# The sum that ends softplus: from VectorE to an accumulating DMA on GpSimd's queue

## What is computed

```
dt = softplus(dt @ W_dt.T + b_dt)             # 512 channels, 512 tokens
A  = -exp(A_log)                              # 512 channels, 16 states
for every token t:                            # for each channel, state n
    h[n] = exp(dt[t] * A[n]) * h[n] + dt[t] * B[t][n] * x[t]
    y[t] = sum over n of h[n] * C[t][n]
out = (y + x * D) * silu(res) @ W_out.T
```

## Time and profile before

| | us |
|---|---|
| median of 3 runs | 2991.44 |
| lowest and highest | 2991.06, 2993.72 |
| the profiled execution | 3002.96 |
| its span, first to last instruction | 3001.2 |

### The profile page before, as it was taken

How to read it: one execution, slowest core, us unless ns; L and a number is a source line. 1 busy time by engine, 2 the same in 40 slices (tenths; PEclk the granted TensorE clock), 3 DMA queues, 4 the chain that set the end, 5 groups by cost and what they waited for, 6 DMA issues and landing times.

```text
span 3001.2 us, 37634 instructions
## 1 busy us (share of the span) xinstructions
PE 2462.4 (82%) x12744; PEld 1387.2 (46%) x12744; DVE 1979.7 (66%) x2957; ACT 1852.0 (62%) x3346; POOL 1731.5 (58%) x1416
## 2 busy tenths in 40 slices
PE   5777679998689998998989898988898879866772
PEld 3444457764444454445444544454444544442331
DVE  4778744543366766776767677766767676778887
ACT  3456723346477785766667667775677667755752
POOL 1000054417657786777688759775876686544555
PEclk9888879999899999998989899999999989988896
DMA  4000158854545565545554455446544653366666
GB/s 142 22 18 5 49 167 236 242 174 69 94 116 108 109 142 130 113 99 111 135 113 100 108 129 110 85 95 141 114 86 94 133 110 81 85 134 138 158 158 144
DMA packets 281152, 344.83 MB, mean 115 GB/s; under 512 B 81600, under 2 KB 210510, under 8 KB 280960
## 3 DMA queue, kind: packets, MB, share of 16 engines
q0 software_dynamic: 84224, 176.19, 32.1%
q1 hardware_dynamic: 174224, 144.67, 16.6%
q10 hardware_dynamic: 22512, 21.57, 2.1%
HBM read 198.10 MB, written 26.80 MB: 75 GB/s over the span
## 4 chain that ended last, share of the span: by engine, by line
PE 44%; ACT 17%; issue 13%; DVE 13%; POOL 7%; DMA 4%; SPq 2%; another core or an unknown queue 0%; DVEq 0%; POOLq 0%; ACTq 0%
PE bank L1763 7%; PE bank L1752 6%; PE bank L1714 5%; PE bank L1899 4%; PE bank L1873 3%; PE bank L1928 3%; PE bank L1821 3%; DVE bank L1532 3%; ACT PT L1018 3%; POOL arena L1643 3%; PE bank L1775 3%; ACT Pr L998 2%; POOL acc_sb L1621 2%; DMA arena<-bc_dram 2%; PE bank L1998 2%
## 5 line engine op out<-in xcount | busy, mean ns | idle before, releaser
L1643 POOL TENSOR_TENSOR arena<-arena 128x512 f32<-128x512 f32 x512 | 859.8, 1738 | 169.7 <-DMA arena<-bc_dram 153.5
L1227 DVE TENSOR_REDUCE negmax<-bank 128x1 f32<-128x512 f32 x512 | 341.2, 681 | 258.7 <-PE bank L1752 257.8
L1621 POOL DMA_INDIRECT acc_sb<-ybuf,slot_idx x256 | 422.1, 1649 | 141.5 <-DMA ybuf<-arena 63.4
L1135 ACT ACTIVATE bank<-arena,A_sb 128x512 f32<-128x512 f32 x512 | 356.6, 699 | 223.5 <-DVE arena L1537 187.8
L1649 POOL TENSOR_TENSOR arena<-arena 128x512 f32<-128x512 f32 x192 | 279.0, 1453 | 323.5 <-DVE arena L1532 290.6
L1752 PE MATMUL bank<-Kp,Qp 64*128 64x512 f32 x1024 | 405.6, 683 | 70.5 <-ACT Pr L998 65.6
L1763 PE MATMUL bank<-ident,Pr 128*128 128x128 f32 x2048 | 353.4, 298 | 127.0 <-ACT PT L1018 63.8
L1532 DVE TENSOR_TENSOR_SCAN bank<-bank,arena 128x512 f32<-128x512 f32 x320 | 390.8, 1221 | 90.2 <-ACT bank L1135 53.3
L998 ACT ACTIVATE Pr<-bank,negmax 128x512 f32<-128x512 f32 x512 | 354.4, 692 | 154.8 <-DVE negmax L1227 138.4
L1018 ACT COPY PT<-bank 128x512 f32<-128x512 f32 x512 | 301.3, 588 | 204.9 <-PE bank L1763 189.9
L1763 PEld LDWEIGHTS bank<-ident,Pr 128*128 128x128 f32 x2048 | 228.9, 147 | 306.5 <-issue 106.3
(11 more groups left out here) (213 smaller groups left out, 3883.2 us busy)
## 6 DMA issues: line engine op xcount, KB each, us to landing
arena<-arena POOLq DMA_DIRECT2D x256, 512.0 KB, 5.4
arena<-bc_dram SPq DMA_DIRECT2D x256, 256.0 KB, 4.2
ybuf<-arena ACTq DMA_DIRECT2D x64, 256.0 KB
arena<-in_w_gate SPq DMA_DIRECT2D x64, 128.0 KB
arena<-in_w_up SPq DMA_DIRECT2D x64, 128.0 KB
arena<-in_w_down SPq DMA_DIRECT2D x64, 128.0 KB
arena<-in_X SPq DMA_DIRECT2D x8, 512.0 KB, 7.1
s_sb<-in_X SPq DMA_DIRECT2D x8, 512.0 KB, 9.1
```

The lines of the kernel that those rows point to most:

```text
L1135: act.activation(bank[DECAY[g % 2]][:, :], dt_sb[:, size_slot(b, cb), :], ACT.Exp, scale=A_sb[:, cb, n:n + 1]).then_inc(ssm_decay, 1)
L1227: dve.tensor_reduce(negmax[:, m % RING_STAT:m % RING_STAT + 1], bank[m % RING_S_ATT][:, :], AX.X, ALU.max, negate=True).then_inc(att_max, 1)
L1621: pool.indirect_dma_start(acc_sb[:, i, :], None, ybuf, bass.IndirectOffsetOnAxis(ap=slot_idx[:, b * TILES + i, k:k + 1], axis=0), bounds_c ...
L1643: pool.tensor_tensor(st_sb[:, g % RING_S, :], u_sb[:, size_slot(b, cb), :], B_sb[:, load % RING_BC, :], ALU.mult).then_inc(ssm_input, 1)
```

## The change

ACT now clips at zero when it writes `dt_sb` (Relu in place of Identity). DVE's L1517 is gone. In its place POOL waits for ACT's logarithm and issues, for each block, one DMA that adds 128x512 of `u_sb` onto `dt_sb` (256 KB; two for a part, 32 in all). The decays and DVE's product L1523 wait for these DMAs to land. `state_inputs` has a piece more: the sum stands beside the step that L1517 stood beside, and the product and `ssm_d` stand one step later than they did.

```diff
--- before.py
+++ after.py
@@ state_inputs
                 E.ssm_soft(b, part)
                 yield True
+                E.ssm_add(b, part)
+                yield True
                 E.ssm_u(b, part)
                 yield True
@@
+    def sized(b, part):
+
+        return 16 * (CB * b + sum(SIZE_PARTS[part]))
@@ ACT, ssm_abs
-                act.activation(dt_sb[:, size_slot(b, cb), :], bank[SIDE][:, :], ACT.Identity, bias=chan_sb[:, cb, DCONV + 1:DCONV + 2]).then_inc(ssm_raw, 1)
+                act.activation(dt_sb[:, size_slot(b, cb), :], bank[SIDE][:, :], ACT.Relu, bias=chan_sb[:, cb, DCONV + 1:DCONV + 2]).then_inc(ssm_raw, 1)
@@ ACT, decay
-                    w.wait_ge(ssm_dt, len(SIZE_PARTS) * b + PART_OF[cb] + 1)
+                    w.wait_ge(ssm_dt, sized(b, PART_OF[cb]))
@@ DVE
             def ssm_u(self, b, part):
-                runs, use = size_runs(b, part), len(SIZE_PARTS) * b + part
-                w.wait_ge(ssm_raw, CB * b + sum(SIZE_PARTS[part]))
-                w.wait_ge(ssm_soft, 2 * use + 2)
-                for own, _ in runs:
-                    dt, u = whole(dt_sb[:, own, :]), whole(u_sb[:, own, :])
-                    ins = dve.scalar_tensor_tensor(dt, dt, 0.0, u, ALU.max, ALU.add)
-                ins.then_inc(ssm_dt, 1)
-                w.wait_ge(ssm_dt, use + 1)
+                runs = size_runs(b, part)
+                w.wait_ge(ssm_dt, sized(b, part))
                 w.wait_ge(ssm_xs, CB * (b + 1))
@@ POOL
+            def ssm_add(self, b, part):
+
+                first, count = SIZE_PARTS[part]
+                w.wait_ge(ssm_raw, CB * b + first + count)
+                w.wait_ge(ssm_soft, 2 * (len(SIZE_PARTS) * b + part) + 2)
+                for cb in range(first, first + count):
+                    slot = size_slot(b, cb)
+                    pool.dma_start(dt_sb[:, slot, :], u_sb[:, slot, :], accum_op=ALU.add).then_inc(ssm_dt, 16)
```

More of the change, by code:

```diff
@@ L123, in ssm_soft, with ssm_add @@
     def ssm_soft(self, b, part): pass
+    def ssm_add(self, b, part): pass
     def ssm_u(self, b, part): pass
```

## The result

The changed kernel takes 3024.40 us in the median of 5 runs (3015.32 to 3034.63), beside 2991.44 us (2987.89 to 2997.20, 5 runs) for the kernel before on the same chip. The ratio is 1.0105, 95% interval 1.0076 to 1.0134. The forecast was 2996 us with a range up to 3007 us. The loss has the sign of the rival "POOL held", and it is some seven times the forecast loss of 4.6 us.

A forecast was written before the change was run, and what follows sets the result against it. No one engine was taken to bound it; the chain ran 44% over PE, 17% ACT, 13% DVE. Start +3.3, batch 1 +0.5, batches 2 to 6 -0.5, batch 7 +1.3: +4.6 us on 2991.4, 2996 us; range up to 3007 us.

The forecast's parts named there:

- POOL held: Rival, slower: POOL waits for the logarithm with gather, inputs and products queued behind; 3004 us; chance 0.35, shared with a start above 6 us.
- Batches 3 to 6 read alike: Middle batches: batch 2, part 0 was worked out and taken to stand for the rest; batches 2 to 6 together -0.5 us.
- the ten free parts: Batches 2 to 6, two parts each: L1517 off the chain, dt landed 2.6 us before the product; -0.5 us, between -4 and +2.
- The stretching that I had counted as gone with L1517: DVE: L1517 takes 1.2 us alone, 2.22 or 2.34 us beside POOL's inputs; the excess was to go with it.
- Batch 1, +0.5 us: Batch 1, chain on POOL: POOL's lateness just fits its margin, DVE gains L1517's 2.34 us; +0.5 us, between -3 and +4.
- 6.8 us of margin: Batch 1: step 64's input ended at 1098.8, its scan began at 1105.55; POOL, about 6 us late, was to fit.
- The start, +3.3 us: Batch 0, nothing covers: L1143 2.85 us late by the landing, plus 0.4 us for part 1; bounds +1.5 and +5.
- The landing, 5.4 us: Every part: from the logarithm's end to dt landed, after two DMA issues; 5.4 us, low end 3.9, high end 6.3.
- the 9.6 us of the longest L1659: Longest landing of a 512 KB add in the trace; landings near it would reach DVE at batches 2 to 6 too.
- Batch 7, +1.3 us: Batch 7, DVE on the chain: product waits for landing, then takes 1.22 us, delaying scan 444 and mask; bounds 0 and +2.9.
- Relief carries: Rival, faster: DVE freed of L1517 and its waits pulls other engines along; 8 us gained, 2983 to 2985 us; chance 0.2.
- signs named as "wrong": DVE waiting for landing in the loop, POOL's inputs releasing scans behind a part, or every batch shorter by a microsecond or more.

The follow-up runs named there:

- mid_p0: The kernel before with the new DMAs and the later product and `ssm_d` only at part 0 of batches 2 to 6: 3012.6 us, ratio 1.0031.
- moved: The kernel before with L1517, the product and `ssm_d` one step later, no DMA: 3032.1 us, ratio 1.0088.
- no_land: The changed kernel with small DMAs onto a spare tile in place of the sum, nobody waiting for their landing: 3021.7 us, ratio 1.0058 to the kernel before.
- small_land: The changed kernel with small DMAs in place of the sum, decays and product waiting for them to land: 3013.2 us, ratio 1.0059 to the kernel before.
- u_late: The kernel before with L1517 and the product one step later, `ssm_d` at its old step, no DMA: 3021.5 us, ratio 1.0056.
- hold_only: The kernel before with POOL waiting for the logarithm beside the step of L1517, issuing nothing: 3010.6 us, ratio 1.0028.
- hold_issue: The kernel before with POOL waiting for the logarithm, then issuing two small DMAs that nobody waits for: 3022.2 us, ratio 1.0050.
- only_b1: The kernel before with the change at batch 1 only, both parts: 3000.8 us, ratio 1.0028.
- no_sum: The kernel before without L1517, with Relu on ACT and the sum left out, no DMA: 2995.7 us, ratio 0.9975.

## Why the prediction was wrong, step by step

**"Batches 3 to 6 read alike" and the ten free parts: this step failed, and with 17 us it is the largest.** I worked out part 0 of batch 2, found the dt landed 2.6 us before the product, and let it stand for ten. For that one part it held: in the changed kernel the product starts there at 1379.9 without a wait, 2.4 us after the landing. Elsewhere DVE waits for the landing: 3.56 us at part 1 of batch 2, 1.49 us at part 0 of batch 5 and 0.3 us at two more; at the other six there is no wait. Three things were missed.

First, part 1 of batch 2. Part 1 is readied one step before its batch needs it, and here the landing was slow as well (below). Batch 2, part 1, in the kernel before: logarithm, sum, product, `AT` of attention (L1242), scan 128, and PE's matmuls that need `AT`.

```profile
1392.72 1.06 ACT L1113 ACTIVATE arena<-arena 128x1024 f32<-128x1024 f32 x1
...
1397.12 1.20 DVE L1517 SCALAR_TENSOR_TENSOR arena<-arena 128x1024 f32<-128x1024 f32 x1
...
1398.35 2.17 DVE L1523 TENSOR_TENSOR arena<-arena 128x1024 f32<-128x1024 f32 x1
...
1402.31 0.68 DVE L1242 TENSOR_TENSOR AT<-bank,inv_bc 128x512 f32<-128x512 f32 x1
...
1402.91 1.22 DVE L1532 TENSOR_TENSOR_SCAN arena<-bank,arena 128x512 f32<-128x512 f32 x1
...
1404.15 7.07 PE L1821 MATMUL bank<-Wpost_sb,AT 128*128 128x256 f32 x32
```

The same place in the changed kernel:

```profile
1395.70 1.06 ACT L1120 ACTIVATE arena<-arena 128x1024 f32<-128x1024 f32 x1
...
1397.30 1.77 POOL L1638 DMA_DIRECT2D arena<-arena  x2 [8.96 <-ACT arena L1120]
...
1405.58 3.23 DVE L1524 TENSOR_TENSOR arena<-arena 128x1024 f32<-128x1024 f32 x1 [3.56 <-DMA arena<-arena]
...
1408.74 0.68 DVE L1249 TENSOR_TENSOR AT<-bank,inv_bc 128x512 f32<-128x512 f32 x1
...
1409.34 1.21 DVE L1533 TENSOR_TENSOR_SCAN arena<-bank,arena 128x512 f32<-128x512 f32 x1
1409.47 10.21 PE L1831 MATMUL bank<-Wpost_sb,AT 128*128 128x256 f32 x32 [2.69 <-DVE AT L1249]
```

From the start of the logarithm to scan 128 it was 10.2 us and is 13.6 us. DVE waits 3.56 us for the landing, the product then takes 3.23 us in place of 2.17 us, and PE, which had no idle time here before, waits 2.69 us behind both.

Second, the product's own duration. I priced it at 1.22 us at its new place. At part 0 of batch 3 it stands at 1677.27 and takes 2.92 us, while POOL, released from its wait, does inputs and products in a row:

```profile
1675.40 1.22 DVE L1533 TENSOR_TENSOR_SCAN bank<-bank,arena 128x512 f32<-128x512 f32 x1
...
1677.27 2.92 DVE L1524 TENSOR_TENSOR arena<-arena 128x1024 f32<-128x1024 f32 x1
```

Before, L1517 had met POOL there and taken 2.80 us, and the product behind it 1.23 us. The stretching that I had counted as gone with L1517 passed to the product. Over all parts that is 34.9 - 23.7 = 11.2 us, 42% of what DVE shed. The Trainium skill (SBUF — State Buffer, section "SBUF: two separate sides") has a DVE instruction with two SBUF inputs and a POOL instruction that reads SBUF lock each other out of a shared port pair; the trace agrees, with 1.2 against 2.9 and 3.2 us for the same product. I had cited it for the forecast's stretched L1517 and should have applied it to the instruction that takes its place.

Third, `ssm_d`. I gave its later place no price at all, and it costs at both parts. At batch 3, part 1, its 1.33 us stand ahead of an exponential of attention (L1005), and PE waits for that:

```profile
1705.18 1.33 ACT L1150 ACTIVATE arena<-arena,chan_sb 128x512 f32<-128x512 f32 x2
...
1706.41 0.68 ACT L1005 ACTIVATE Pr<-bank,negmax 128x512 f32<-128x512 f32 x1
...
1707.23 1.12 PE L1762 MATMUL bank<-Kp,Qp 64*128 64x512 f32 x2 [1.00 <-ACT Pr L1005]
```

Before, PE had no idle time at that place. At part 0 of batch 4 it is the same, here in `mid_p0`, where L1154 is `ssm_d` and L1009 the exponential:

```profile
1964.39 1.35 ACT L1154 ACTIVATE arena<-arena,chan_sb 128x512 f32<-128x512 f32 x2
...
1965.62 0.71 ACT L1009 ACTIVATE Pr<-bank,negmax 128x512 f32<-128x512 f32 x1
...
1967.03 0.63 PE L1784 MATMUL bank<-ident,Pr 128*128 128x128 f32 x4 [1.37 <-ACT PT L1029]
```

Scan 254 is 1.2 us later after scan 253 than in either trace of before, in every kernel with `ssm_d` late at part 0 (`moved`, `mid_p0`, `no_land`, `small_land` and both traces of the changed kernel), and in no other. The forecast had weighed POOL and the landing at part 0, and not this. What the rest of the 0.31% of `mid_p0` is stays open.

Back to batch 3: the stretch from scan 192 to scan 196 holds the same work in all kernels on PE, DVE and ACT, as the counts show. Here it is in the kernel before, in `u_late` (where `ssm_d` is at its old step) and in the changed kernel; the columns are the window, its length, busy times of PE, PEld, DVE, ACT and POOL with their counts, PE's granted clock, DMA share and GB/s:

```profile
1689.83:1703.72 13.89, 12.33 (x90) 7.04 (x88) 10.05 (x13) 11.37 (x25) 11.08 (x10) 1.00 0.62 133
```

```profile
1699.01:1712.89 13.88, 12.32 (x90) 7.03 (x88) 10.05 (x13) 11.33 (x25) 11.07 (x10) 1.00 0.61 133
```

```profile
1701.45:1719.38 17.93, 15.39 (x90) 8.65 (x88) 10.05 (x13) 11.43 (x25) 16.59 (x13) 0.81 0.66 133
```

It is 4.0 us longer. The granted clock, 2.4 GHz throughout in the first two, is 0.81 on average in the third, so at 1.2 GHz for some 40% of it, and PE works 3.1 us longer on the same matmuls. The microsecond of idle time comes first and the fall after it. But the one doesn't always bring the other: in the second trace of the changed kernel PE has the same 1.00 us of idle time before the same matmul, the clock stays at 2.4 GHz, and the stretch is 1.7 us longer. So the idle time costs 1.7 us or less for itself, and the rest of the 4.0 us goes with the clock, whose fall no run explains. The loss comes with `ssm_d` in each of the six traces that have it late here (1.2 to 4.0 us), and in none of the others.

**Batch 1, +0.5 us: the step failed at the place that was compared.** POOL's lateness was set against scan 64, with 6.8 us of margin. But scans 60 and 61 come first, and so does `AT`. From the changed kernel: logarithm, the DMAs, the product, `AT`, scan 60 and the matmuls that need `AT`.

```profile
1073.18 1.06 ACT L1120 ACTIVATE arena<-arena 128x1024 f32<-128x1024 f32 x1
...
1074.79 1.78 POOL L1638 DMA_DIRECT2D arena<-arena  x2 [6.26 <-ACT arena L1120]
...
1082.99 1.35 DVE L1524 TENSOR_TENSOR arena<-arena 128x1024 f32<-128x1024 f32 x1 [3.76 <-DMA arena<-arena]
...
1084.26 0.68 DVE L1249 TENSOR_TENSOR AT<-bank,inv_bc 128x512 f32<-128x512 f32 x1
...
1084.86 1.21 DVE L1533 TENSOR_TENSOR_SCAN arena<-bank,arena 128x512 f32<-128x512 f32 x1
...
1084.99 7.33 PE L1831 MATMUL bank<-Wpost_sb,AT 128*128 128x256 f32 x26 [4.91 <-DVE AT L1249]
```

The landing took 8.2 us from the first issue, so DVE waited 3.76 us and PE 4.91 us. At scan 60 `moved` and `u_late` are 2.1 us late and the changed kernel 4.8 and 5.2 us: place and landing.

What holding POOL does here isn't what the rival "POOL held" said. In `hold_only` scan 61 is 3.2 us late, but POOL's input isn't what it waits for. The addition ahead of it on DVE waits for PE:

```profile
1095.18 0.42 DVE L1248 TENSOR_TENSOR s_sb<-bank,s_sb 128x256 f32<-128x256 f32 x1 [6.18 <-PE bank L1826]
```

From scan 60 to scan 61 PE's granted clock is 1.00 in the first trace of before and the stretch takes 4.2 us; it is 0.71 and 5.9 us in the second, 0.60 and 7.7 us in `hold_only`, and 0.73 and 0.58 with 5.7 and 7.1 us in the two of the changed kernel. So up to half of those 3.2 us is seen without any change, and what sets the clock there stays open. At scan 63 `hold_issue` is 8.0 us late, 4.8 us more than `hold_only`, and there it is DVE: its sum and product of part 1 take 4.99 and 3.52 us, against 2.34 and 1.34 us before. In this trace POOL's next input and product run beside them, pushed back by the two issues. The changed kernel has no sum to be stretched, and its product of that part takes 2.40 us. The forecast's comparison of POOL's lateness with the margin of 6.8 us asked the wrong engine. `only_b1` confirms the size of the loss at batch 1: +0.28%.

**The start, +3.3 us: right mechanism, too small.** It was 5.2 and 6.0 us, a little over the upper bound of 5. The 0.4 us that the forecast added for part 1 didn't come: scan 4 follows scan 0 as fast as before (-0.3 us). Logarithm, DMAs, product, and first scan:

```profile
797.85 1.06 ACT L1120 ACTIVATE arena<-arena 128x1024 f32<-128x1024 f32 x1
...
799.50 1.86 POOL L1638 DMA_DIRECT2D arena<-arena  x2 [3.75 <-ACT arena L1120]
...
806.59 1.23 DVE L1524 TENSOR_TENSOR arena<-arena 128x1024 f32<-128x1024 f32 x1 [12.89 <-DMA arena<-arena]
...
811.22 1.22 DVE L1533 TENSOR_TENSOR_SCAN arena<-bank,arena 128x512 f32<-128x512 f32 x1 [3.07 <-ACT bank L1142]
```

The term that was mis-sized is the landing: 7.7 us from the end of the logarithm to the product, where I took 5.4 us and 6.3 us as the high end. The rest of the step, |a| and a slipping ahead and `ssm_d` behind the product, came as worked out: the delay is 5.2 us where 2.85 us were forecast ahead of part 1, and those 2.3 us more are what 7.7 exceeds 5.4 by.

**The landing, 5.4 us: right at eleven parts and wrong at five, where DVE does 25.7 of its 29.4 us of waiting.** From issue to landing of a part's two DMAs, at batch 3 part 0 and at batch 2 part 1, and then what queue q1, on which SP's loads go, moved in the 5 us from the issue in the second case (packets, MB, share of 16 engines); in the first case that queue moved nothing:

```profile
DMA to landing us min/median/max: 3.4/3.8/4.3
```

```profile
DMA to landing us min/median/max: 4.8/6.2/7.7
...
q1 hardware_dynamic: 218, 0.21, 12.6%
```

At the ten parts at which queue q1 moved nothing the landings are 3.3 to 4.5 us, and from the end of the logarithm to the second landing it is 5.4 to 5.6 us, as I took. At the start, at both parts of batch 1, at part 1 of batch 2 and at part 1 of batch 7, q1 moved 0.11 to 0.63 MB in those 5 us, and the second DMA took 6.5, 7.6, 8.5, 7.7 and 7.7 us. At part 0 of batch 7 q1 moved 0.08 MB, and the landings stayed at 3.4 and 4.4 us. I had the 9.6 us of the longest L1659 as a remote case, when the trace of before could have been asked what moved on the queues at each of the 16 places. The small DMAs of `small_land` show the same: 2.2 to 2.5 us at part 0 of batch 2, 2.8 and 5.9 us at part 1. The Trainium skill (DMA: Bandwidth & Descriptors, section on queues, rings and completion order) says that each DMA engine goes round the queues it has work for, a packet at a time. That would make a landing longer whenever another queue has work, as seen; that it is the reason here no run shows.

**Batch 7, +1.3 us: right mechanism, too small.** It was some 4 us. The product was forecast to wait for landing and then take 1.22 us. It waited 1.52 us and took 3.33 us, so scan 444 is 3.4 us late and not 1.2 us; the term that was mis-sized is again the product's duration. A mask of the trees stands behind it, for whose product PE waits 4.04 us, where it had waited 1.02 us before:

```profile
2814.03 1.77 POOL L1638 DMA_DIRECT2D arena<-arena  x2 [7.09 <-ACT arena L1120]
...
2819.00 3.33 DVE L1524 TENSOR_TENSOR arena<-arena 128x1024 f32<-128x1024 f32 x1 [1.52 <-DMA arena<-arena]
...
2824.12 0.74 DVE L1493 SCALAR_TENSOR_TENSOR PT<-bank,need_sb,AT 128x512 f32<-128x512 f32 x1
...
2824.91 2.08 PE L1938 MATMUL bank<-PT,xaT 128*128 128x512 f32 x2 [4.04 <-DVE PT L1493]
```

**Relief carries: the mechanism exists.** `no_sum` gives 0.25%, some 7.5 us, about the 8 us of that rival. I had held it to be hidden at the middle batches; there its trace is 4.7 us shorter than the mean of before over the five stretches, of which 3.6 us lie at batches 2 and 3, where the traces of before themselves differ by 3.5 and 2.1 us, so whether it was hidden stays open. In the changed kernel 11 of the 27 us never became free, and the rest is less than what the waits and delays above cost.

**What held**: landings of 3 to 5.4 us where nothing else moves; POOL idle for the logarithm ahead of L1638, 112.3 us in 15 times, 7.5 us each where I had said 5; the first scan later. Of the signs named as "wrong", DVE waiting for landing in the loop came: 16.5 us in 8 places.

What stays open: how much of the last 0.31% to 0.46% is DVE's wait and how much the data of the new DMAs meeting other transfers; batch 2, part 1 shows 4 us of it at one place. A DMA of full size that nobody waits for wasn't tried. And the granted clock: it is a little lower in the changed kernel (0.909 to 0.916 over its runs, 0.918 in the profile of before), as cause or as consequence of the longer waits.

## What to carry over

Work out each place at which a change acts, not one of a kind: the part that was worked out held, and the others lost for three different causes. Give everything that the change moves a price, also what looks too small to matter: `ssm_d`, 1.3 us of ACT, got none. And look for the first consumer behind a wait, since it sets the margin. Ask the trace what every queue moves at each place before a DMA's landing is given one price, and give a moved instruction the duration that it has beside its new neighbours. Taking an instruction off a half idle engine gained here about a quarter of its time (by the interval a tenth to a half), but handing it to a DMA put a wait for landing in its place, on the same engine; leaving the operation out by another form of the function gained on both engines.

## What the runs showed of the hardware

- A 256 KB add within SBUF by POOL's queue landed 3.3 to 4.5 us after its issue with no other queue moving, and up to 8.5 us with another queue moving; a 24 KB one 2.2 to 2.5 us, and up to 6.1 us. The Trainium skill (DMA: Bandwidth & Descriptors, section on the anatomy of one DMA on the GpSimd path) gives about 2.0 us plus bytes over 436 GB/s, by estimate 2.06 us for the small one and 2.6 us for the add: near the trace for the first, too little for the second.
- The same product of 128x1024 on DVE took 1.2 us alone and up to 3.3 us beside POOL's inputs and products. With the sum taken away (`no_sum`), the product behind it took over its place and its longer times.
- The same idle microsecond of PE was followed by a fall of the granted clock in one trace (mean 0.81, the stretch 4.0 us longer) and by none in another (1.00, 1.7 us longer).
